# A perceiver layer on one core: row sums of the self-attention by a column of ones on TensorE, the shift of the maximum on ScalarE, and new orders around them

## The reference, cut to what matters

```python
# cross-attention, 8 heads of 64, onto 25088 context rows
x = x + xattn(layernorm(x), ctx, ctx)
# self-attention over 256 rows, 16 heads of 32, with an additive bias
k_, v_, q_ = split(layernorm(x) @ w_in.T)
logits = einsum(q, k) / sqrt(32) + bias
x = x + softmax(logits) @ v
# 8 experts, the best two of each row weighted, hidden size 1024
x = x + moe(layernorm(x))
```

## Time and profile before

| | before |
|---|---|
| median of 3 runs | 1588.63 us (1588.28 to 1592.83) |
| profiled execution | 1592.57 us, its span 1590.9 us |
| PE busy | 1517.5 us (95%) |
| DVE, ACT, POOL busy | 1318.4, 1266.1, 939.6 us |
| TensorE clock, mean of the span | 0.982 of full speed |
| HBM read | 111.96 MB |

### The profile page before, as it was taken

One profiled execution on the slowest core, in us unless ns is written; L12 is line 12 of the kernel. 1 busy time (PEld: TensorE's weight loads), 2 busy tenths in 40 slices (PEclk: granted clock), 3 DMA queues, 4 the chain that ended last, 5 costly groups with the idle time before them and its releaser, 6 DMA issues.

```text
span 1590.9 us, 47821 instructions
## 1 busy us (share of the span) xinstructions
PE 1517.5 (95%) x17752; PEld 1252.5 (79%) x17752; DVE 1318.4 (83%) x1767; ACT 1266.1 (80%) x3078; POOL 939.6 (59%) x946
## 2 busy tenths in 40 slices
PE   6999999999999999999999999999989566999998
PEld 5787888888888888888888888888878445777776
DVE  7788888888988888888888898888888776767665
ACT  4888888888888888888888888888878655655554
POOL 5667787787877877878778787787775121000000
PEclk9999999999999999999999999999999787999999
DMA  4376656656556466555565655656656858555550
GB/s 179 75 138 109 138 115 136 140 110 138 124 122 143 107 137 136 120 134 115 135 141 109 138 128 120 141 108 136 134 105 130 165 137 248 201 203 199 208 205 27
DMA packets 460018, 220.22 MB, mean 138 GB/s; under 512 B 433840, under 2 KB 439984, under 8 KB 453184
## 3 DMA queue, kind: packets, MB, share of 16 engines
q1 hardware_dynamic: 459680, 219.26, 57.7%
q10 hardware_dynamic: 288, 0.27, 0.0%
HBM read 111.96 MB, written 0.56 MB: 71 GB/s over the span
## 4 chain that ended last, share of the span: by engine, by line
PE 83%; DVE 7%; DMA 4%; ACT 2%; issue 2%; POOL 2%; SPq 0%; POOLq 0%; DVEq 0%; ACTq 0%
PE ps_proj L1301 50%; PE ps_proj L1513 10%; PE ps_s L1351 8%; PE ps_o L1369 8%; PE ps_o L1536 5%; DMA pt_s<-p_s 3%; PE ps_proj L1330 1%; DVE p_s L943 1%; DVE cmax L930 1%; POOL ctx_s L416 1%; DVE wsp L1146 1%; DMA ctx_f<-ctxt_dram 1%; ACT prob L718 0%; PE ps_o L1271 0%; POOL p_s L495 0%
## 5 line engine op out<-in xcount | busy, mean ns | idle before, releaser
L1301 PE MATMUL ps_proj<-ctx_s,wk_s 128*128 128x256 f16 x4032 | 481.6, 273 | 4.1 <-ACT ps_proj L569 3.6
L1301 PE MATMUL ps_proj<-wv_s,ctx_s 128*128 128x256 f16 x4032 | 480.6, 273 | 1.9 <-ACT ps_proj L571 1.9
L1301 PEld LDWEIGHTS ps_proj<-ctx_s,wk_s 128*128 128x128 f16 x4032 | 380.5, 98 | 67.0 <-issue 24.6
L1301 PEld LDWEIGHTS ps_proj<-wv_s,ctx_s 128*128 128x128 f16 x4032 | 380.0, 98 | 63.8 <-issue 12.0
L416 POOL TENSOR_TENSOR ctx_s<-t_f,ctx_s 128x512 f16<-128x512 f32 x192 | 261.2, 1370 | 281.0 <-ACT ctx_s L517 281.0
L615 ACT ACTIVATE prob<-ps_s,nmax 128x256 f32<-128x256 f32 x776 | 356.5, 475 | 11.6 <-DVE nmax L937 11.2
L930 DVE TENSOR_REDUCE cmax<-ps_s 128x4 f32<-128x1024 f32 x194 | 237.4, 1224 | 125.1 <-PE ps_s L1351 124.9
L943 DVE SCALAR_TENSOR_TENSOR p_s<-prob,p_s 128x1024 f16<-128x1024 f32 x196 | 321.5, 1640 | 0.7 <-ACT p_s L626 0.7
L416 POOL TENSOR_TENSOR ctx_s<-ctx_f,ctx_s 128x512 f16<-128x512 f32 x144 | 215.9, 1499 | 11.4 <-ACT ctx_s L512 6.9
L626 ACT ACTIVATE p_s<-prob 128x1024 f16<-128x1024 f32 x196 | 206.7, 1055 | 8.0 <-DMA pt_s<-p_s 1.3
L1369 PE MATMUL ps_o<-v_s,pt_s 128*128 128x64 f16 x4704 | 172.3, 194 | 19.9 <-DMA pt_s<-p_s 19.7
(11 more groups left out here) (175 smaller groups left out, 1783.1 us busy)
## 6 DMA issues: line engine op xcount, KB each, us to landing
ctx_f<-ctxt_dram SPq DMA_DIRECT2D x48, 1024.0 KB, 5.6
wst<-w_dram SPq DMA_DIRECT2D x96, 512.0 KB, 4.8
pt_s<-p_s SPq DMA_TRANSPOSE x408, 3.1
w_in_f<-w_in_dram SPq DMA_DIRECT2D x3, 1024.0 KB, 5.5
tisa<-tisa_scores SPq DMA_DIRECT2D x12, 256.0 KB, 5.8
w_f<-wk_dram SPq DMA_DIRECT2D x2, 512.0 KB, 6.2
ctx_f<-ctxt_dram SPq DMA_DIRECT2D x2, 512.0 KB, 7.5
w_f<-wv_dram SPq DMA_DIRECT2D x1, 1024.0 KB, 10.9
```

Source lines behind the costliest of these rows:

```text
L1301: ins = pe.matmul(ps_proj[:, bank(h, role), sub * QUARTER:(sub + 1) * QUARTER], lhsT, rhs, start=(fresh and sub == 0 and t == 0 and i == 0 ...
```

## The change

Six edits, all in the end of the cross-attention and in the self-attention:

1. The row sums of the exponentials are no longer read out by ScalarE. `weigh2` has 16 more matmuls a pair, each with a column of ones (128x1), into `ps_o`; `attended` takes the reciprocal of that, behind `pv2_done`.
2. The shift of the maximum is a ScalarE instruction ahead of the exponentials; GpSimd writes the constants `ones` and `shift` once.
3. `pt2_s` has four buffers, so the transposes of pair p wait for `weigh2` of pair p-4 (those of pairs 2 and 3 for the projection of V, whose weights lie in the same memory).
4. ScalarE issues the load of `w_in_f[V]`, in the step of chunk 47, in its first half; SyncE did it, late in the second half.
5. `last_step`: TensorE takes `scores(48, 2)` ahead of `weigh(47, 3)`; VectorE makes the low halves of the Q weight ahead of `last_o(1)`, not between the layernorm and `x_lows`.
6. Self-attention: TensorE projects only K of the second group ahead of `scores2(0)`, the second half of V behind `scores2(1)` and the last group behind that; the halves of these results are taken later on ScalarE and VectorE.

```diff
@@ SyncE
-                    for i, at, used in ((K, (NCH - 3, 0), LAST), (Q, (NCH - 2, 0), NCH), (V, (NCH - 2, 2), NCH)):
+                    for i, at, used in ((K, (NCH - 3, 0), LAST), (Q, (NCH - 2, 0), NCH)):
...
-                if p >= 2:
-                    sp.wait_ge(pv2_done, 2 * (p - 1))
+                if p >= 4:
+                    sp.wait_ge(pv2_done, 2 * (p - 3))
+                elif p >= 2:
+                    sp.wait_ge(v2_done, 2)
                 for k, split in enumerate((p2_high, p2_low)):
                     sp.wait_ge(split, p + 1)
-                    sp.dma_start_transpose(pt2_s[:, p % 2, k, :, :], p2_s[:, p % 2, k, :]).then_inc(turned2[p % 2], 16)
+                    sp.dma_start_transpose(pt2_s[:, p % 4, k, :, :], p2_s[:, p % 2, k, :]).then_inc(turned2[p % 4], 16)
@@ GpSimd
+            pool.wait_ge(pv_done, CROSS_PV)
+            pool.memset(ones[:, :], 1.0)
+            pool.memset(shift[:, :], P_SHIFT).then_inc(ones_ready, 1)
@@ ScalarE
                         if h == 0:
+                            act.wait_ge(ctx_low, UNITS * NCH)
+                            act.dma_start(w_in_f[V][:, :, :], w_in_dram[V]).then_inc(w_in_loaded[V], 16)
                             act.wait_ge(unit_done, units_through(2 * LAST))
...
-                act.wait_ge(nmax2_done, p + 1)
+                act.wait_ge(max2_done, p + 1)
+                if p >= 2:
+                    act.wait_ge(exp2_done, p - 1)
+                act.activation(nmax2[:, 1, p % 2, :], nmax2[:, 0, p % 2, :], ACT.Identity, bias=shift[:, :]).then_inc(nmax2_done, 1)
                 if p >= 2:
                     act.wait_ge(p2_low, p - 1)
+                act.wait_ge(nmax2_done, p + 1)
...
-                                             bias=nmax2[:, p % 2, 2 * j + r:2 * j + r + 1], accum_out=lsum2[:, h // 8, r, h % 8:h % 8 + 1])
+                                             bias=nmax2[:, 1, p % 2, 2 * j + r:2 * j + r + 1])
@@ VectorE
                 last_base(1)
+                w_in_lows(Q, 0)
+                w_in_lows(Q, 1)
                 link(last_o(1))
...
             normalised(stream)
-            w_in_lows(Q, 0)
-            w_in_lows(Q, 1)
...
-                dve.wait_ge(max2_done, p + 1)
-                dve.tensor_scalar(nmax2[:, p % 2, :], nmax2[:, p % 2, :], P_SHIFT, None, ALU.add).then_inc(nmax2_done, 1)
...
-                dve.wait_ge(exp2_done, 4 * half + 4)
-                link(dve.reciprocal(lsum2[:, half, :, :], lsum2[:, half, :, :]))
                 dve.wait_ge(pv2_done, 8 * half + 8)
+                link(dve.reciprocal(lsum2[:, half, :, :].rearrange("p r h -> p (r h)"), ps_o[:, half, 0:2 * 8]))
...
-            kq_lows(1)
             for p in range(PAIRS):
                 logits(p)
-                if p < 2:
-                    kq_lows(2 + p)
+                if p == 0:
+                    kq_lows(1)
                 if p == 2:
+                    kq_lows(2)
                     v2_lows(0)
+                if p == 3:
                     v2_lows(1)
+                    kq_lows(3)
@@ TensorE
+                        for s in range(2):
+                            for a in range(2):
+                                pe.matmul(ps_o[:, g // 8, col:col + 1], pt2_s[:, p % 4, a, 4 * j + 2 * r + s, :], ones[:, :],
+                                          start=(s == 0 and a == 0), stop=(s == 1 and a == 1))
```

More of the change, by code:

```diff
@@ L139, in layer @@
         w_in_f = [sb(f"w_in_f{i}", [P, DT, D], F32, w_in) for i in range(3)]
+        w_in_s = [None, None, None]
+        w_in_s[V] = [sb(f"w_in_s{V}{k}", [P, DT, D], F16, w_in) for k in range(2)]
         w_in.close()
@@ L142, in layer @@
         prob2 = sb("prob2", [P, 4, 2 * T], F32)
-        pt2_s = sb("pt2_s", [P, 2, 2, 8, P], F16)
-        w_in_s = [None, None, None]
-        for i in (V, Q, K):
+        pt2_s = sb("pt2_s", [P, 4, 2, 8, P], F16)
+        for i in (Q, K):
             w_in_s[i] = [sb(f"w_in_s{i}{k}", [P, DT, D], F16) for k in range(2)]
@@ L151, in layer @@
         p2_s = sb("p2_s", [P, 2, 2, 4 * T], F16)
-        nmax2 = sb("nmax2", [P, 2, 4], F32)
+        nmax2 = sb("nmax2", [P, 2, 2, 4], F32)
+        ones = sb("ones", [P, 1], F16)
+        shift = sb("shift", [P, 1], F32)
         lsum2 = sb("lsum2", [P, 2, 2, 8], F32)
@@ L178, in layer @@
         w_in_high, w_in_low = [sem(f"w_in_high{i}") for i in range(3)], [sem(f"w_in_low{i}") for i in range(3)]
-        turned2 = [sem(f"turned2{i}") for i in range(2)]
+        turned2 = [sem(f"turned2{i}") for i in range(4)]
         piece_loaded, out_stored = [sem(f"piece_loaded{i}") for i in range(4)], sem("out_stored")
@@ L725, in p2_highs @@
                 if p >= 2:
-                    act.wait_ge(turned2[p % 2], 32 * (p // 2))
+                    act.wait_ge(turned2[(p - 2) % 4], 32 * ((p - 2) // 4) + 32)
                 act.activation(p2_s[:, p % 2, 0, :], prob2[:, 2 * (p % 2):2 * (p % 2) + 2, :].rearrange("p h c -> p (h c)"),
@@ L742, in _ @@
                 exps2(p)
-                if p < 2:
-                    kq_highs(2 + p)
+                if p == 2:
+                    v2_highs(1)
                 p2_highs(p)
                 if p == 1:
+                    kq_highs(2)
                     v2_highs(0)
-                    v2_highs(1)
+                if p == 2:
+                    kq_highs(3)
             piece_highs(0, 0, range(3))
@@ L1406, in last_step @@
                 weigh(LAST - 1, 2, 1 - odd)
+                scores(LAST, 2, odd)
                 weigh(LAST - 1, 3, 1 - odd)
-                scores(LAST, 2, odd)
                 scores(LAST, 3, odd)
@@ L1424, in _, with project_kq @@
             pe.wait_ge(x_split, 2)
-            def project_kq(e):
+            def project_kq(e, parts=(K, Q)):
                 if e == 0:
@@ L1431, in project_kq @@
                 for n, i in enumerate((K, Q)):
-                    for t in range(DT):
-                        for k, (a, b) in enumerate(THREE):
-                            ins = pe.matmul(KQ_BANK[e][:, n * T:(n + 1) * T], w_in_s[i][a][:, t, e * P:(e + 1) * P], x_s[b][:, t, :],
-                                            start=(t == 0 and k == 0), stop=(t == DT - 1 and k == 2))
-                ins.then_inc(kq_done, 1)
+                    if i in parts:
+                        for t in range(DT):
+                            for k, (a, b) in enumerate(THREE):
+                                ins = pe.matmul(KQ_BANK[e][:, n * T:(n + 1) * T], w_in_s[i][a][:, t, e * P:(e + 1) * P],
+                                                x_s[b][:, t, :], start=(t == 0 and k == 0), stop=(t == DT - 1 and k == 2))
+                if Q in parts:
+                    ins.then_inc(kq_done, 1)
             def project_v2(r):
@@ L1461, in weigh2 @@
             def weigh2(p):
-                pe.wait_ge(turned2[p % 2], 32 * (p // 2) + 32)
+                pe.wait_ge(turned2[p % 4], 32 * (p // 4) + 32)
                 if p == 0:
                     pe.wait_ge(v2_low, 2)
-                    pe.wait_ge(kq_low, DT)
+                    pe.wait_ge(ones_ready, 1)
+                if p % 4 == 0:
+                    pe.wait_ge(kq_low, 3 + p // 4)
                 for j in range(2):
@@ L1472, in weigh2 @@
                                 col = r * QUARTER + (g % 8) * HD
-                                ins = pe.matmul(ps_s[:, g // 8, col:col + HD], pt2_s[:, p % 2, a, 4 * j + 2 * r + s, :],
+                                ins = pe.matmul(ps_s[:, g // 8, col:col + HD], pt2_s[:, p % 4, a, 4 * j + 2 * r + s, :],
                                                 v2_s[b][:, s * D + g * HD:s * D + (g + 1) * HD],
@@ L1478, in _ @@
             project_kq(0)
-            project_kq(1)
+            project_kq(1, (K,))
             scores2(0)
+            project_kq(1, (Q,))
             project_kq(2)
+            project_v2(0)
+            scores2(1)
+            project_v2(1)
             project_kq(3)
-            project_v2(0)
-            project_v2(1)
-            scores2(1)
             weigh2(0)
```

10 lines of the change are left out of this document (6 added, 4 removed).

## The result

The median went from 1590.34 us (1588.28 to 1592.83, six runs) to 1581.06 us (1578.71 to 1583.00, six runs): ratio 0.9939, 95% interval 0.9926 to 0.9952, so 7.6 to 11.8 us less. Timed again later beside three other kernels, the changed kernel had 1582.92 against 1591.07, ratio 0.995 (0.9936 to 0.9963). The forecast was 1579.7, in a range of 1576 to 1586: faster, in the main by the mechanism named, and 1.4 us too low.

What follows compares the result with a forecast made beforehand. The prediction took the chain of waits ahead of the experts as the bound: chunk 48, second layernorm, self-attention. 2.5 + 1.26 + 5.9 - 0.8 = 8.9 us, off the median 1588.63, gave 1579.7, range 1576 to 1586.

Steps and rivals of the forecast that it cites:

- Chunk 48: Last cross-attention chunk: moving V's load and taking scores(48, 2) ahead starts the maximum of group 2 2.5 us earlier.
- price at the new place: Chunk 47's first half, where ScalarE now issues V's load: taken as 0, bounds 0 and 2.5 us.
- Layernorm: Second layernorm to first projection: moving the low halves of Q's weight off this path saves 1.26 us.
- Self-attention: First projection to last `weigh2`: the new schedule starts the copy of pair 7 5.9 us earlier; bounds 3.0 to 8.0.
- half clock that I had put on pair 4: Self-attention: if `scores2(2)` runs at half clock (1.47 against 0.83), all from pair 4 on is 0.6 us later.
- The end: Behind the last transpose: 16 more matmuls cost 0.5 us and the reciprocal 0.28, together -0.8.
- Table load: Ahead of pair 0's exponentials: formerly hidden, now costs its 1.28 us on the path; no drain shows.
- The experts: Stretch behind the attention: keeps its 254 us, since TensorE has no gap there.
- The first rival: Chunk 48: the load doesn't matter, transposes crowd each other; 0.7 us instead of 2.5, time 1581.5; chance 0.13.
- The second: Self-attention: exponentials stay at 2.08 or `weigh2(0)` comes 2 us later; gain 3.5, time 1582.1; chance 0.15.
- The third: Self-attention: the copy loop over two buffers eats the lead; gain 1, sum 4 us, time 1584.6; chance 0.09.
- The clock: Projections: TensorE at its lower clock doubles their 3 x 5.41 us, making the kernel slower, 1595.9; chance 0.03.

Runs made afterwards that it cites:

- load_back: Changed kernel with the load of V's weight back in SyncE's queue, late in chunk 47's step: 1586.14 us against 1582.92.
- q_lows_behind: Changed kernel with Q's weight low halves back between layernorm and halves of x: layernorm to first projection 4.53 us against 3.27; not timed.
- early_table: Changed kernel with a one-column exponential behind the halves of x, loading the table early: first projection to last `weigh2` 43.69 us against 44.33; not timed.
- scores_ahead: Changed kernel with the scores of pairs 4 and 5 ahead of `weigh2(0)`: first projection to last `weigh2` 44.44 us against 44.33; not timed.

## Why the prediction was right, step by step

- *Chunk 48, forecast 2.5*: group 2 came 2.53 earlier, and A is 3.0 shorter, since the last transposes landed in 4.50 instead of 4.98 as well, which no term of the forecast holds. The load is the cause of 1.9 to 2.3 us of group 2 and 2.1 to 2.6 of A (load_back, twice); the order of the scores brings 0.4 to 0.8. The premise that "the load is the only foreign traffic in that row" overlooked the `instruction` packet. I took 0 for the price at the new place; the sign of it that I had named, TensorE waiting in the chunk loop for a transpose, came in eight of nine traces, but only 0 to 0.7 us reached the next maximum.
- *Layernorm, forecast 1.26*: measured 1.26, and undone by q_lows_behind alone.
- *Self-attention, forecast 5.9*: 5.0. The schedule held within 0.4 at every copy named, even where it was moved by 6 us, and the copy of pair 7 was 0.4 better than forecast (the half clock that I had put on pair 4 did not come). The term was mis-sized in its last link: for the loop a transpose was given 3.2 to 4.1, and the last one was then taken like the 3.1 of before, where it took 4.36, with an `instruction` packet in its flight. Copy 7 came 6.3 earlier, the landing is 1.28 longer, and 5.0 are left.
- *Its parts*: the shift on ScalarE is worth about 1.9 and the four buffers 1.2. I had written that "the four buffers cost and bring nothing by themselves". That was wrong: it overlooked that pair 2's first transpose can start at 19.6 (copy 18.55 and 1.06), and that with two buffers its place is free only behind `weigh2(0)`, which I had put at 20 myself. The sums moved to TensorE, worth 0.4 us a pair on ScalarE, are worth nothing at the end.
- *The end, forecast -0.8*: -0.67. 16 more matmuls 0.42 (0.026 each), and the reciprocal 0.29.
- *Table load*: 1.28 us ahead of pair 0, as worked out; no drain shows behind it. At the end it is worth 0.64 (early_table), not 1.28.
- *The experts*: 254 us stretches with 251.3 and 251.6 busy, as forecast.

The first rival (the load doesn't matter) is out by load_back. The second too: the exponentials take 1.70 without the read-out, and the first `weigh2` starts at 20.2, for 20.0 forecast. The third is wrong in size: the loop over two buffers holds up pair 6 by 0.51 us, and whether it would bind in a better order is open (scores_ahead). The clock stayed at 1.00 in the experts, and the projections ran at full clock.

The 8.7 against 8.9 is closer than the parts: chunk 48 gave 0.5 more than forecast, the self-attention 0.9 less, the end cost 0.1 less. That these nearly cancel is luck. So is part of the time: the sum was put on the median of three runs, 1588.63, and with three more the median of before is 1590.34. That is 1.7 us of the level, more than the whole miss of 1.4.

## What to carry to other kernels

Look in SyncE's queue for a plain load issued just ahead of a transpose that ends a phase: moved some 15 us up, to where the transposes beside it have slack, a 1 MB load gave back 2.1 to 2.6 us of that phase, for at most 0.7. When an instruction is added to save time elsewhere, count its price to the last link: the column of ones won 1.9 us at the last copy, lost 1.3 of it in the last landing and 0.6 behind it. When a transfer is longer than its neighbours, look in the DMA view for a packet of kind `instruction` in its flight before explaining it by the schedule. And ask of each small VectorE instruction between a maximum and its exponential whether GpSimd works beside it; on ScalarE it costs a steady 0.3.
